# A selective-scan chunk pipeline with its preparation reordered, and two of its four gates moved from the vector engine to ScalarE and GpSimd

## What is computed

```
xs, z = split(x @ in_w.T)                  # 512 channels each
xc    = silu(cb + causal 4-tap convolution of xs)
dt, B, C = split(xc @ xp_w.T)              # 16, 16 and 16 wide
delta = softplus(dt @ dt_w.T + dt_b)
h[t]  = h[t-1] * exp(delta * A) + delta * xc * B      # 512 x 16 states
y     = sum_n h * C + xc * D_skip
out   = (y * silu(z)) @ out_w.T            # "the gate" is the product y * silu(z)
x     = layernorm(out + x) * ln_w + ln_b
```

## Time and profile before

| | |
|---|---|
| median of 3 runs | 8295.75 us (8295.15 to 8297.27) |
| the profiled execution, its own time | 8298.0 us |
| its span (first to last instruction) | 8296.2 us |
| mean granted TensorE clock | 0.894 |
| busy: DVE / POOL / PE / ACT | 95% / 84% / 79% / 67% of the span |
| q1 DMA queue | 45.7% of 16 engines' span |

### The profile page before, as it was taken

How to read it: one execution, slowest core, us unless ns; L and a number is a source line. 1 busy time by engine, 2 the same in 40 slices (tenths; PEclk the granted TensorE clock), 3 DMA queues, 4 the chain that set the end, 5 groups by cost and what they waited for, 6 DMA issues and landing times. The chain is left out here.

```text
span 8296.2 us, 75437 instructions
## 1 busy us (share of the span) xinstructions
PE 6530.6 (79%) x21028; PEld 2528.0 (30%) x21028; DVE 7849.2 (95%) x7411; ACT 5545.2 (67%) x9589; POOL 6983.9 (84%) x3444
## 2 busy tenths in 40 slices
PE   5777777787778777787777877887777877775888
PEld 2222222232223222222222322232222322222555
DVE  8999999999999999999999999999999999996776
ACT  5676776777766776667766777667766777663444
POOL 3898889988898888988899888988889888985555
PEclk8989899989989899898999889898999888987999
DMA  6454454444554454554545445454555445451110
GB/s 181 116 118 109 104 127 115 117 115 113 127 118 110 100 121 115 120 122 108 126 115 117 105 109 126 116 125 103 121 119 119 109 104 122 115 118 52 39 38 30
DMA packets 566028, 909.25 MB, mean 110 GB/s; under 512 B 58368, under 2 KB 200192, under 8 KB 564352
## 3 DMA queue, kind: packets, MB, share of 16 engines
q1 hardware_dynamic: 565632, 904.73, 45.7%
HBM read 715.55 MB, written 188.94 MB: 109 GB/s over the span
## 5 line engine op out<-in xcount | busy, mean ns | idle before, releaser
L905 POOL TENSOR_TENSOR hc<-h,crep 128x1024 f32<-128x1024 f32 x2048 | 4782.2, 2360 | 714.3 <-PE acc L474 633.4
L1033 DVE TENSOR_TENSOR_SCAN h<-dA,carry,bu 128x512 f32<-128x512 f32 x3072 | 3755.0, 1264 | 0.4 <-ACT carry L638 0.4
L1018 DVE TENSOR_TENSOR bu<-durep,B_all 128x1024 f32<-128x1024 f32 x2048 | 2480.8, 1211 | 188.2 <-PE B_all L456 168.2
L629 ACT ACTIVATE dA<-drep,cur 128x512 f32<-128x512 f32 x4096 | 2618.7, 711 | 0.6 <-DMA drep<-delta_dram 0.3
L456 PE MATMUL B_all<-dtc,spread_b 128*128 128x512 f32 x2048 | 1308.0, 724 | 1460.8 <-DVE bu L1018 1458.5
L638 ACT COPY carry<-h 128x4 f32<-128x4 f32 x1023 | 199.4, 195 | 1713.0 <-DVE h L1033 1711.6
L474 PE MATMUL acc<-hc,gather 128*32 128x512 f32 x8192 | 1284.9, 703 | 5.5 <-POOL hc L905 5.5
L1033 DVE TENSOR_TENSOR_SCAN h<-dA,bu 128x512 f32<-128x512 f32 x1024 | 1192.4, 1203 | 6.9 <-ACT dA L629 6.8
L498 PE MATMUL work<-xT,inw 128*128 128x512 f32 x2048 | 1119.6, 697 | 93.1 <-ACT xT L649 82.7
L456 PEld LDWEIGHTS B_all<-dtc,spread_b 128*128 128x128 f32 x2048 | 360.0, 208 | 2144.9 <-DVE bu L1018 2057.0
L508 PE MATMUL work<-xs,taps 128*128 128x512 f32 x2048 | 950.3, 607 | 0.0
(11 more groups left out here) (179 smaller groups left out, 6807.8 us busy)
## 6 DMA issues: line engine op xcount, KB each, us to landing
drep<-delta_dram SPq DMA_DIRECT2D x1024, 256.0 KB, 6.4
durep<-du_dram SPq DMA_DIRECT2D x1024, 256.0 KB, 7.2
crep<-c_dram SPq DMA_DIRECT2D x1024, 64.0 KB, 6.7
delta_dram<-za SPq DMA_DIRECT2D x64, 1024.0 KB, 4.2
du_dram<-relu SPq DMA_DIRECT2D x64, 1024.0 KB, 5.3
x_res<-xbuf SPq DMA_DIRECT2D x64, 512.0 KB, 3.8
xbuf<-x_res SPq DMA_DIRECT2D x64, 512.0 KB, 5.4
xc<-xbuf SPq DMA_DIRECT2D x63, 512.0 KB, 4.3
```

What stands on the lines that cost most here:

```text
L629: act.activation(dA[:, 4 * (s % 2) + k, :], drep[q % 2][:, k, :], ACT.Exp, scale=cur[:, p_, 4 * s + k:4 * s + k + 1]).then_inc(da_ready, 1)
L905: pool.tensor_tensor(hc[:, pair, :], h[:, pair, :], crep[:, j:j + 1, :].to_broadcast([P, 2, T]), ALU.mult).then_inc(hc_ready, 1)
L1018: dve.tensor_tensor(bu[:, 2 * k:2 * k + 2, :], durep[q % 2][:, 2 * k:2 * k + 2, :], B_all[:].unsqueeze(1).to_broadcast([P, 2, T]), ALU.mul ...
L1033: dve.tensor_tensor_scan(h[:, r, :], dA[:, r, :], bu[:, k, :], start, ALU.mult, ALU.add).then_inc(scanned, 1)
```

## The change

Three things are done.
1. **Gates.** DVE keeps the gates of q = 0 and q = 2. For q = 1 (at s = 10) and q = 3 (at s = 2 of the next turn) ACT copies `acc` into `sums[:, 0]` ahead of its exp (`take_sums`), and POOL multiplies it into `sz` behind `times_c` of the same s. `sums` is also the target of `squares`, so each waits for the other.
2. **Skip terms.** They are no longer the first matmul of their quarter but stand ahead of the sum of group 1, 3, 1, 1 of it (`SKIP_AT`), that is of groups 1, 7, 9 and 13. `load_x` waits for the second one, and so now for the first pair of group 7.
3. **Preparation.** On PE the z projection goes from s = 8, 9 to 7, 8, the transposes of x from 10 to 9, the xs projection from 11, 12 to 10, 11, and the convolutions from 13, 14, 15, 0 to 12 to 15. On ACT the copy of xT goes from s = 11, behind the exp and the root guess, to s = 10, ahead of the exp; z copies go to 8, 9, xs copies to 11, 12, convolution copies to 13, 14, 15, 0; tanh and silu(z) from s = 1 to 0. On POOL the SiLU product goes from s = 2 to 1. The order of fills of the two work banks is counted anew.

```diff
+    SKIP_AT = (1, 3, 1, 1)
...
             def load_x(n):
                 c = ready(n % CH)
                 if n >= 2:
-                    sp.wait_ge(summed, 2 * (NG * (n - 2) + QS) + 1)
+                    sp.wait_ge(summed, 2 * (NG * (n - 2) + 2 * QS - 1) + 1)
...
             def sum_states(at, p_):
...
-                if s % QS == 0:
-                    skip_term(n, p_, s // QS)
+                q = s // QS
+                if s % QS == 0 and positive(DB * n + q):
+                    pe.wait_ge(acc_read, DB * n + q)
+                if s % QS == SKIP_AT[q]:
+                    skip_term(n, p_, q)
...
             def project_out(m, p_, j):
                 if j == 0:
+                    pe.wait_ge(gated, 2 * (m + 1))
...
-                        if s == 0:
-                            convolve(nxt, 3)
...
-                        if s in (8, 9):
-                            project_in(nxt, 2 * (s - 8), 1)
-                            project_in(nxt, 2 * (s - 8) + 1, 1)
+                        if s in (7, 8):
+                            project_in(nxt, 2 * (s - 7), 1)
+                            project_in(nxt, 2 * (s - 7) + 1, 1)
...
-                            if s == 10:
+                            if s == 9:
                                 transpose_x(g + 2)
...
-                            if s in (13, 14, 15):
-                                convolve(g + 2, s - 13)
+                            if s >= 12:
+                                convolve(g + 2, s - 12)
...
+            def take_sums(n, q):
+                act.wait_ge(summed, 2 * (NG * n + QS * (q + 1)))
+                if positive(2 * n + q // 2):
+                    act.wait_ge(gated, 2 * n + q // 2)
+                squares_ahead = n if q == 1 else min(n, TOT - 1)
+                if positive(squares_ahead):
+                    act.wait_ge(squared, squares_ahead)
+                act.copy(sums[:, 0, :], acc[:]).then_inc(acc_read, 1)
...
                 for s in range(NG):
                     keep_states(group(g, s - 1))
+                    if s == 10 and not is_last(g) and g < TOT - 2:
+                        copy_xT(g + 2)
+                    if s == 2 and not is_first(g):
+                        take_sums(g - 1, DB - 1)
+                    if s == 10:
+                        take_sums(g, 1)
                     exp(group(g, s + 1), here if s + 1 < NG else other)
...
+            def gate(n, p_, q):
+                if q == 1:
+                    pool.wait_ge(z_done, n + 1)
+                pool.wait_ge(acc_read, DB * n + q + 1)
+                pool.tensor_tensor(sz[:, p_, q, :], sums[:, 0, :], sz[:, p_, q, :], ALU.mult).then_inc(gated, 1)
...
                     times_c(group(g, s))
+                    if s == 2 and not is_first(g):
+                        gate(g - 1, other, DB - 1)
+                    if s == 10:
+                        gate(g, 1 - other, 1)
...
                     scan(at, ph, 0)
-                    if s == 2 and not is_first(g):
-                        gate(g - 1, other, DB - 1)
-                    if s in (6, 10, 14):
+                    if s in (6, 14):
                         gate(g, here, (s - 6) // 4)
```

More of the change, by code:

```diff
@@ L69, in mamba_layers @@
     C_DB, C_CB = 0, DB
+    SKIP_AT = (1, 3, 1, 1)
+    FILL_BANK = {"xp": 0, "dt0": 1, "dt1": 0, "dt2": 1, "dt3": 0, "out0": 0, "out1": 1, "tr0": 0, "tr1": 1}
+    FILL_BANK.update({f"{name}{e}": e % 2 for name in ("z", "xs", "c") for e in range(4)})
     xv = xbuf.rearrange("(c t p) d -> c p t d", t=NT, p=P)
@@ L190, in is_last @@
             return isinstance(g, int) and g == TOT - 1
[L192 to L212, removed]
-        def fill(b, n, name):
[L216 to L220, removed]
@@ L222, in mamba_layers, with place, place_head @@
-        LAST_OUT = (fill0(TOT, "out") + 1, fill1(TOT, "out") + 1)
+        fill_at, filled = {}, [0, 0]
+        def place(n, *names):
+            for name in names:
+                b = FILL_BANK[name]
+                fill_at[b, n, name] = filled[b]
+                filled[b] += 1
+        def place_head(n):
+            place(n, "tr0", "tr1", "xs0", "xs1", "xs2", "xs3", "c0", "c1", "c2", "c3")
+        place_head(0)
+        place(0, "xp", "dt0", "dt1", "dt2", "dt3", "z0", "z1", "z2", "z3")
@@ new lines, in mamba_layers @@
+        place_head(1)
+        for n in range(1, TOT + 1):
+            if n < TOT:
+                place(n, "xp", "dt0", "dt1", "dt2", "dt3")
+            if n >= 2:
+                place(n - 2, "out0", "out1")
+            if n < TOT:
+                place(n, "z0", "z1", "z2", "z3")
+            if n < TOT - 1:
+                place_head(n + 1)
+        place(TOT - 1, "out0", "out1")
+        def fill(b, n, name):
+            return fill_at[b, n, f"{name}{b}" if name in ("tr", "out") else name]
@@ L224, in out_fill @@
         def out_fill(b, m):
-            if isinstance(m, int) and m == TOT - 1:
-                return LAST_OUT[b]
-            return fill(b, m + 2, "out")
+            return fill(b, m, "out")
         def group(g, s):
@@ L460, in skip_term @@
                     pe.wait_ge(skip_w, 16 * layer_of(n) + 16)
-                if positive(DB * n + q):
-                    pe.wait_ge(acc_read, DB * n + q)
-                pe.matmul(acc[:], skip[:, q, :], xc[:, p_, q, :], start=True, stop=False, skip_group_check=True)
+                pe.matmul(acc[:], skip[:, q, :], xc[:, p_, q, :], start=False, stop=False, skip_group_check=True)
             def sum_states(at, p_):
@@ L473, in sum_states @@
                         pe.wait_ge(hc_ready, 2 * G + k // 2 + 1)
-                    ins = pe.matmul(acc[32 * k:32 * k + 32, :], gather[:], hc[:, 4 * (s % 2) + k, :], start=False,
+                    ins = pe.matmul(acc[32 * k:32 * k + 32, :], gather[:], hc[:, 4 * (s % 2) + k, :], start=s % QS == 0,
                                     stop=s % QS == QS - 1, skip_group_check=True)
@@ L571, in _ @@
             turn_piece(2)
-            for e in range(3):
+            for e in range(DB):
                 convolve(1, e)
@@ L818, in _ @@
             copy_piece(2)
-            for e in range(2):
+            for e in range(3):
                 copy_conv(1, 1, e)
@@ L857, in turn @@
                     if not is_last(g):
-                        if s == 9 and is_first(g):
+                        if s == 8 and is_first(g):
                             act.wait_ge(weights_saved, 48)
-                        if s in (9, 10):
-                            copy_z(n, other, 2 * (s - 9))
-                            copy_z(n, other, 2 * (s - 9) + 1)
+                        if s in (8, 9):
+                            copy_z(n, other, 2 * (s - 8))
+                            copy_z(n, other, 2 * (s - 8) + 1)
                     if not is_first(g):
@@ L884, in _ @@
             turns(act, turn)
+            take_sums(TOT - 1, DB - 1)
             for j in range(2):
@@ L997, in _ @@
             turns(pool, turn)
+            gate(TOT - 1, 1, DB - 1)
             mean(TOT - 1)
@@ L1154, in _ @@
             turns(dve, turn)
-            m = TOT - 1
-            gate(m, 1, DB - 1)
 class Fp4:
```

35 lines of the change are left out of this document (16 added, 19 removed).

## The result

The changed kernel takes 8390.03 us in the median of 4 runs (8383.68 to 8398.42) against 8296.22 us for the kernel before on the same chip: a ratio of 1.0114 (95% interval 1.0096 to 1.0131), 94 us slower. The prediction said 8322 with a range up to 8385. The sign is right, the size is more than three times what was forecast (94 against 26), and the time lies above the range. The rival that comes nearest in size is the fourth (8380, slower by more).

What follows compares the result with a forecast made beforehand. DVE, busy 95%, was taken as the bound, with POOL's chain beside it almost without room. +0.85 - 0.45 = +0.4 a turn, +25 over 62 turns and +1 at the end, gave 8322 us, range 8238 to 8385.

Steps and rivals of the forecast that it cites:

- Rival 4: Slower by more: half clock on into the xs projection, or a landing over 5; 8380, chance 0.07.
- POOL's chain: POOL's work from softplus to group product 12, without idle time; 1.3 of slack, lengthened by the gate of q = 1.
- T14: Start of DVE's first scan of group 14; at 65.8 after T5 before, forecast at 66.6.
- half product 12: First half of POOL's group product 12, which the scan at T14 waits for; from 64.5 to 66.5 after T5.
- The load of x: At s = 9, issued 34.8 after T5, landing at 39.1; PE waits 4.4, DVE stalls 2.2 in group 10.
- The output copy frees the second bank late: PE's z projection from s = 7 waits for ACT's copy until 24.0; group 9 stalls 0.8, not 0.41.
- du is waited for: Next turn's du lands at 79.6, wanted by DVE for group 0 at 78.9: a stall of 0.7.
- The stalls of groups 3 and 12: DVE's waits for B of 0.56 (x projection) and 1.39 (xs projection waiting for xT); both were to go.
- Stretch B: Part of a turn from T14 to the next T5: 50.5 to 50.05, -0.45.
- stretch A: Part of a turn from T5, start of group 5's scan, to T14: 65.8 to 66.65, +0.85.
- Its first pair is done at 44.0.: First pair of PE's sum 8, wanted by POOL's product 10 at 43.2: POOL's chain 0.8 later.
- The port rival: POOL gates stop DVE through a shared port for 1.25 each, twice a turn: 8477, chance 0.03.

Runs made afterwards that it cites:

- x_early: Changed kernel with the skip term of q = 1 at group 5, not 7, so the load of x starts three groups earlier: 8294.13 us.
- inw_first: Changed kernel with the next layer's in-projection weights ahead of the load of x in SP's order: 8368.99 us.
- gate1_late: x_early with POOL's gate product of q = 1 moved from s = 10 to s = 14, behind the softplus chain: 8215.38 us.
- q1_dve: x_early with the gate of q = 1 given back to DVE, without its copy and POOL product: 8218.98 us.
- before_delta_first: Kernel before with only SP's loads of delta for q = 0 of the next turn put ahead of the store of du: 8270.74 us.

## Why the prediction was right and wrong

**Right in mechanism at nearly every place.** POOL's chain decides when a turn passes T14: in the changed kernel T14 stands 0.20 behind half product 12 in every turn without a layer change; A is 65.9 in most turns of x_early, and the time moves with a product put in (+57 us) and with one taken out (-79 and -75 us). The gate of q = 1 off DVE is worth nothing at that place, and less than nothing. The load of x is issued at 34.7 (34.8), waited for by PE until 39.2 (39.1), and makes B late in group 10 by 2.0 in the mean (2.2). The output copy frees the second bank late: 0.70 in most of the 49 turns that have this stall (0.8). du is waited for in 61 turns and not in 24. The stalls of groups 3 and 12 fall to 0.1 in the mean. Stretch B: -0.49 (-0.45). Not seen was the second path from POOL's gate, by the variance, the root guess and the copy of xs; it counts in 15 turns of x_early and little in the changed kernel.

**Wrong in size, in stretch A: +2.07 and not +0.85 a turn.** Two terms of the sum failed, and a third was read from a turn that is not the mean.

1. "Its first pair is done at 44.0." I took half of the sum's time for the first of its two pairs. The signals of the two pairs come 0.06 apart at the end of the sum. Without the layer changes sum 8 starts at 42.8 in the mean (I had 43.1), takes 1.60, and POOL starts product 10 at 0.15 behind its end: at 44.5 and not at 44.0, after a wait of 1.3 and not 0.8. T14 follows by 22.75, so A is 67.3 in the mean, 0.65 above my 66.65. In 62 turns that is near 40 us. The same error is in my reading of the earlier trace rows: SP's issue at 4012.98 stands 1.09 behind the start of a sum of 1.06, and not 0.6 behind its half. The turn at T5 = 4049.74 agrees with 66.65 by luck: there the clock came back during sum 8, which took 1.22 from 42.6, so that its end fell where I had put its half. The transposes took 1.97, all at the lower clock, in 48 of 62 turns.
2. The layer changes are in no term. I moved eight loads behind the load of x and asked who waits for them, but did not follow the ninth: the weights, which are issued behind them in 3 of 64 turns. That is 21 us by inw_first.
3. The turn of the kernel before from which I took A has 65.8; the mean of the turns 2 to 61 is 65.6. That is near 11 us.

Together these are 72 us where 68 lie between 8322 and 8390; the other 4, of the opposite sign, are not split further. Rival 4 (0.07) comes near in size, at 8380, but not by what it names: only 2 of the 63 loads of x took clearly over 5 to land (6.3 and 6.7), and in 42 of the 57 turns without a layer change the first xs projections run wholly at full clock, in the others at most 0.3 longer. So its closeness is luck too, and the range ended 5 us short.

**The port rival is out** (it had 0.03): scans at 1264 ns before and after, products bu with a median of 1205 to 1215 ns in every run, and the same POOL product costs 79 us or nothing by its place alone (gate1_late against x_early and q1_dve). The Trainium skill's sentence that offloading between DVE and GpSimd may not help ("Perfetto Trace Analysis", Optimizing Scalar/DVE Operations) came true for the gate of q = 1, but by another way than a port, and not for that of q = 3 (-41 us).
The 3.2 us that the fit of the Trainium skill ("DMA: Bandwidth & Descriptors", Anatomy of one DMA) gives as an estimate for the 512 KB of x is below every landing of the kernel after:

```profile
DMA to landing us min/median/max: 4.0/4.4/6.7
```

**Open:** why B is earlier in before_delta_first, and how much of the 79 us of gate1_late belongs to each of the two paths.

## What to carry to other kernels

An engine at 93% need not be the bound: find the chain that releases it at its next buffer, and put moved work where that chain has idle time, not where the work used to stand. When a wait is moved on an in-order queue, write down every instruction behind it, those of one turn in sixteen too, and who asks for each. A price read from one turn is that turn's: look at a dozen before it is multiplied by 62. And a wait that a view puts down to an engine long done belongs to another.

## What was not expected of the hardware

A group of four column-tiled fp32 matmuls signals its first pair late: POOL, released by the first pair, starts 2.08 after the start of a sum that takes 1.94, and the signals of its two pairs are 0.06 apart; at full clock SP's issue stands 1.09 behind the start of a sum of 1.06, which could have told it. And useless matmuls can pay: after 4.2 to 6.8 of standstill PE's transposes took 1.97 in 48 of 62 turns, and 1.09 in nearly all where four matmuls had cut the standstill to 0.9 (median), which was worth 64 us of 8390.
